# One layer of retention and mixture of experts: the fourth x split sooner, steps 7 to 9 reordered, two x1 tiles on GpSimd

## The chip, the cores and the metric

The kernel runs on one core of a Trainium2 chip. The core has TensorE (PE, with its weight loads PEld), VectorE (DVE), ScalarE (ACT), GpSimd (POOL) and SyncE (SP), which only issues transfers here. The metric is the device time in microseconds.

## The reference

Input x is 16 sequences of 256 tokens with 256 channels. The reference computes, in float32:

```
q, k, v, g = x@w_q+b_q, x@w_k+b_k, x@w_v+b_v, x@w_g+b_g      # 8 heads of 32
q, k = rotated by position (sin, cos)
sim = (q k^T / sqrt(32)) * decay mask (causal, gamma_h ** distance)
ret = group norm of (sim v) per head, * gn_weight + gn_bias
x1  = layernorm(x + (silu(g) * ret) @ w_o + b_o)
logits = x1 @ router_w.T ; the best of 8 experts, score = sigmoid(best logit)
routed = expert MLP of x1*score (256 -> 2*512 -> 256, up * silu(gate))
shared = (silu(x1@sh_gate) * (x1@sh_up)) @ sh_down
out = layernorm(x1 + shared + routed)
```

## The kernel before

The 16 sequences are worked on as 8 pairs of 512 tokens (four tiles of 128). A loop over t runs from 0 to 9; what is done in one turn is called step t here. In step t three pairs are on their way at once: pair t is projected to q, k, v and gate, pair a = t - 1 goes through its similarities, values, group norm and output product, and pair f = t - 2 is layer-normed to x1, turned, put through the shared MLP and routed. Steps 3 to 7 are alike; step 8 has no pair to project (a = 7, f = 6), and step 9 has only the shared MLP of pair 7. After step 9 come 39 slots, each one gather of 128 tokens, one expert's MLP and one scatter.

Every engine has its own list of instructions, written out by hand in the order of its function, and runs it strictly in order; engines wait for each other by semaphores (`wait_ge`). An instruction that waits holds up everything behind it on its engine. There is no planner.

Float32 products are made of three passes of a faster format: a value is split into a high part, copied by ACT, and a low part, which DVE or POOL gets by subtraction. For x this is `x_hi(t)` (ACT) and `x_lo(t)` (DVE, line 1191: x_in minus the high part, both in SBUF). Step t splits the x of pair t + 1, behind the variance; in step 2 alone `x_lo(3)` stands almost at the end (line 1622), behind `y_rest(1)` (line 1278) and in front of `shared_sum(0, ...)` (line 1302) and `output_sum(1)` (line 1315), whose result the similarities of pair 2 (line 1820) wait for. In the same step POOL's list ends with `residual` (line 1020), `turn` (line 977) and `down_rest` (line 1053).

The expert weights are split in the same way in steps 3 to 9: `expert_hi(e)` (ACT, line 811), `expert_lo(e, n)` (DVE, line 1335, waits until n high parts are there) and `expert_rest` (POOL, line 1040). They lie where the projection weights, xT and other buffers of the pairs lie, and so SP's `gate_up_in(e)` waits until those are free.

In step 8 the order is: PE four times similarities and values of pair 7, `x1_transposes(6)` (line 1934), `ret_transposes(7)`, `gate_up_shared(6, ...)` (line 1740) with `y_transposes(7)` (line 2012) and `output(7)` (line 2085) in between, `shared_down(6, 0)` (line 2034), `x1_transposes(7)`, `shared_down(6, 1)`. POOL: `group_rstd(7)` (line 1014), `residual(7)`, four scatters of seats (line 1077), `norm_scales(7)` (last instruction line 1035, semaphore nmr_ok). ACT then writes four tiles of x1 (`first_norm`, line 794), and the high part of x1T (line 743). DVE ends step 8 with `plan_early`, `expert_lo(1, 3)`, `shared_sum(6, 0)`, `x1_lo(7)` (line 1241), `shared_sum(6, 1)`, `expert_lo(2, 4)`; step 9 begins with `shared_product(7, 0)` (line 1287, semaphore h_ok), for which PE waits in front of the fifth of its eight groups `gate_up_shared(7, j, i)`. POOL goes from `norm_scales(7)` to `expert_rest(5, 7)`, which waits for the seventh high part: ACT's `expert_hi(5)`, right behind `x1_hi(7)`.

Of the kernel before, what the change touches and what calls it, by code (L numbers as in the profile page):

```python
# [51 lines left out]
HALF_FF = FF // 2  # L52
PARTED = {1: (0,), 2: (1,), 3: (2,), 4: (3, 4), 5: (5,), 6: (6,), 7: (7,)}
SEATS = (EXPERTS - 1) * TOKENS + SLOTS * P
SEAT = 3
# [7 lines left out]
def build(nc, x, w_q, b_q, w_k, b_k, w_v, b_v, w_g, b_g, w_o, b_o, gn_w, gn_b, router_w,  # L63
          gate_up, down, sh_gate, sh_up, sh_down, x_t, b_qk, w_o_t, b_o_col, rotation, squares, token_seats, free_seats, out):
    ctx = ExitStack()
    with ctx:
# [203 lines left out]
        def x1T_duo(f):  # L270

            return duo[0] if f == PAIRS - 2 else x1_duo(f)

        def v_bank(q):
# [21 lines left out]
        class sig:  # L296
# [68 lines left out]
            lnr_ok = new("lnr_ok")  # L365
            nm_ok = new("nm_ok")
            nmr_ok = new("nmr_ok")
            x1_ok = new("x1_ok")
# [137 lines left out]
        def _(sp):  # L506
# [47 lines left out]
            def step(t):  # L554
# [35 lines left out]
                if has(t - 2) and t < PAIRS:  # L590
                    sums_out(t - 2)
# [85 lines left out]
        def _(act):  # L677
# [76 lines left out]
            def shared_act(f, j):  # L754
                act.wait_ge(sig.gu_ps, 2 * FT * f + 2 * j + 1)
                act.wait_ge(sig.h_ok, at(FT * f + j - 1))
                act.wait_ge(sig.h_rest, at(min(FT * f + j - 1, FT * (PAIRS - 2))))
                nc.scalar.activation(s_act[:, j % 2, :], duo[j % 2][:, 0, :], ACT.Silu).then_inc(sig.sact_ok, 1)

# [37 lines left out]
            def expert_hi(e):  # L797

                act.wait_ge(sig.egu_in[e], 16)
                if e < 2:  # L800
                    act.wait_ge(sig.g_ps, KT * PAIRS)
                    act.wait_ge(sig.xT_lo, KT * PAIRS)
                elif e < 4:
# [32 lines left out]
            for t in range(1, PAIRS + 2):  # L836
# [28 lines left out]
                if has(t) and t > 1:  # L865
                    gate_act(t)
                if has(f):
                    if t == PAIRS:
                        expert_hi(1)
# [16 lines left out]
                if has(f):  # L886
# [9 lines left out]
                    if t == PAIRS:  # L896
                        expert_hi(3)
                    shared_act(f, 3)
# [63 lines left out]
        def _(pool):  # L962
# [124 lines left out]
            for t in range(PAIRS + 2):  # L1087
# [35 lines left out]
                if t == PAIRS:  # L1123
                    norm_scales(a)

            pool.wait_ge(sig.plan_ok, 2)
# [60 lines left out]
        def _(dve):  # L1187
# [93 lines left out]
            def shared_product(f, j):  # L1281
# [4 lines left out]
                to = s_act[:, j % 2, :] if h_parts(f) else hT[:, j, :]  # L1286
                nc.vector.tensor_tensor(to, duo[j % 2][:, 1, :], s_act[:, j % 2, :], ALU.mult)\
                    .then_inc(sig.h_ok, 1)
# [8 lines left out]
            def shared_sum(p, i):  # L1297

                dve.wait_ge(sig.dn_ps, 2 * p + i + 1)
                dve.wait_ge(sig.x1_ok, TILES * (p + 1))  # L1300
                dve.wait_ge(sig.zs_out, 16 * p)
# [23 lines left out]

            def moments(p):
                for q in range(TILES):
                    dve.wait_ge(sig.st_ok, TILES * p + q + 1)
# [15 lines left out]
            def last_products(f):  # L1344

                shared_product(f, 0)
                shared_product(f, 1)
                expert_lo(3, 5)
                for j in range(2, FT):
# [173 lines left out]
            for t in range(1, PAIRS + 2):  # L1523
                a, f = t - 1, t - 2
                if t == 2:
                    products(t, 0)
                    products(t, 1)
                elif has(a):
                    masked(a, 0)
                    if t == PAIRS:  # L1530
                        statistics(f, [0, 1])
                    elif has(f):
                        statistics(f)
                        moments(f)
# [40 lines left out]
                if t == 2:  # L1575
                    swap(t, 1)
                elif has(t + 1) and t != 1:
                    x_lo(t + 1)
                if t == PAIRS + 1:
                    last_products(f)  # L1580
                elif has(f):
# [12 lines left out]
                    else:  # L1594
                        group_norm(a, [0])
                        choose(f)
                        group_norm(a, [1])
                        shared_product(f, 1)
                        go_on(f)
                        find_seats(f)  # L1600
                        gated(a)
                        shared_product(f, 2)
                        for i in range(2):
                            output_sum(a, [i])
                            statistics(a, [2 * i, 2 * i + 1])
                        moments(a)
                    shared_product(f, 3)
                    h_low(f, 3)
                    if t == PAIRS:
                        plan_early()  # L1610

                        dve.wait_ge(sig.nmr_ok, PAIRS)
                        expert_lo(1, 3)
                if has(a) and t < PAIRS:
# [118 lines left out]
        def _(pe):  # L1733
# [66 lines left out]
            def similarities(a, quad):  # L1800
# [3 lines left out]
                if quad == 0:  # L1804

                    pe.wait_ge(sig.v_ok, 2 * (a + 1))
                    if a > 1:
                        pe.wait_ge(sig.gate_ok, KT * (a + 1))
                        pe.wait_ge(sig.z_ok, 2 * (a - 1) + 1)
# [97 lines left out]
            def ret_transposes(a):  # L1907
                pe.wait_ge(sig.ident_in, 16 * 2)
                pe.wait_ge(sig.retT_ok, 2 * (a + 1))

                pe.wait_ge(sig.s_diag, 8 * (a + 1))
                if has(a + 1):
                    pe.wait_ge(sig.prod_ok, 4 * (a + 2))
# [6 lines left out]
            def x1_transposes(f):  # L1920
# [16 lines left out]
                if f == PAIRS - 1:  # L1937
                    for q in range(TILES):
                        pe.wait_ge(sig.x1_ok, TILES * f + q + 1)
                        for k in range(KT):  # L1940
# [34 lines left out]
            def gate_up_shared(f, j, i):  # L1975
                if i == 0:
                    if j == 0:
                        pe.wait_ge(sig.x1T_lo, KT * (f + 1))
                        if f == 0:
                            pe.wait_ge(sig.w_lo, 5)  # L1980
                    if j < 2:

                        if has(f + 2):
                            if j == 0:
                                pe.wait_ge(sig.v_ok, 2 * (f + 3))
                            else:
                                pe.wait_ge(sig.gate_ok, KT * (f + 3))
                        elif has(f + 1):
# [3 lines left out]
                    else:  # L1992
                        pe.wait_ge(sig.h_ok, FT * f + j - 1)
                three(duo[j % 2][:, i, :], lambda part, k: wsgu[:, i, part, k, j * P:(j + 1) * P],
                      lambda part, k: x1T[:, part, k, :], KT).then_inc(sig.gu_ps, 1)
# [27 lines left out]
            def shared_down(f, half):  # L2023
# [14 lines left out]
                if half == 0:  # L2038
# [13 lines left out]
                    down_part(0, [FT - 1])  # L2052
                    down_part(1, range(FT)).then_inc(sig.dn_ps, 1)
                else:
                    down_part(2, [FT - 1])
# [50 lines left out]
            for t in range(1, PAIRS + 2):  # L2106
                a, f = t - 1, t - 2
                if has(a):
                    for n in range(4):
                        if t != 2:  # L2110
                            similarities(a, n)
                            if n:
                                values(a, n - 1)
                        if t == 1 and n == 0:
                            router_of_output()
                        if has(t):
                            project(t, n)
                    if t != 2:
                        values(a, 3)
# [10 lines left out]
                if has(t) and t != 1:  # L2130
                    gate_project(t, [1] if t == 2 else range(KT))
                if t == 1:
# [31 lines left out]
                if has(f):  # L2164
                    shared_down(f, 0)
                    if t == PAIRS:
                        x1_transposes(a)
                    shared_down(f, 1)
                if has(a) and t < PAIRS:
# [190 lines left out]
```

## Time and profile before

| | |
|---|---|
| median of 3 runs | 558.79 us (558.39 to 558.9) |
| the profiled execution | 558.9 us, span 557.1 us |
| PE busy | 537.1 us, 96% of the span, 3830 matmuls |
| DVE, ACT, POOL busy | 414.3, 229.6, 337.7 us |
| mean granted clock | 0.987 |

The profile's times are microseconds from the start of the span. Steps 3 to 7 take some 41.5 us each, with PE busy nearly without a break. The page gives the granted TensorE clock in 40 slices of 13.9 us: it is at 9 (of 10) everywhere but in the seventh slice (from 83.6 us), where it is at 6, and the last.

### The profile page before, as it was taken

Reading aid. Unit: us, or ns where it says so; the run is one execution under the profiler, and the core shown is the slowest. Engines: PE = TensorE matmul, PEld = TensorE weight load, DVE = VectorE, ACT = ScalarE, POOL = GpSimd, SP = SyncE. Lnnn points to the kernel's source line nnn. Section 1 sums busy time; section 2 is a strip of 40 time slices with the busy share of each in tenths; the row PEclk is TensorE's granted clock in tenths of the full one; section 3 lists DMA queues with packets and bytes.
Section 4 is the critical chain, followed back from the end, with each engine's and each line's share of the span. In section 5 each row is a group of like instructions: output and inputs, shape, how many; then the busy total and the mean of one; then the engine's idle time right before and its main releaser. Section 6 shows DMA issues by size and latency. Waiting matters only on the chain.

```text
span 557.1 us, 11796 instructions
## 1 busy us (share of the span) xinstructions
PE 537.1 (96%) x3830; PEld 453.8 (81%) x3830; DVE 414.3 (74%) x892; ACT 229.6 (41%) x410; POOL 337.7 (61%) x330
## 2 busy tenths in 40 slices
PE   8999995999999999999999889999999999999994
PEld 6777894789789789789788678888888888888884
DVE  5896988787987987987977778767866666666664
ACT  4435550355453353353354855133333333333331
POOL 1956674395495385785485385616786556566644
PEclk9999996999999999999999999999999999999998
DMA  8920503403623503603366713855586665565651
GB/s 267 318 94 3 188 3 111 153 2 50 238 94 63 204 1 51 216 1 117 113 251 243 289 53 118 277 181 188 189 195 202 198 189 177 175 198 194 198 181 38
DMA packets 46555, 83.82 MB, mean 150 GB/s; under 512 B 11361, under 2 KB 30577, under 8 KB 46481
## 3 DMA queue, kind: packets, MB, share of 16 engines
q1 hardware_dynamic: 38720, 64.52, 35.0%
q0 software_dynamic: 6112, 15.40, 10.4%
q10 hardware_dynamic: 1664, 3.15, 1.6%
q8 instruction: 33, 0.54, 0.4%
q14 instruction: 26, 0.21, 0.2%
HBM read 61.11 MB, written 22.34 MB: 150 GB/s over the span
## 4 chain that ended last, share of the span: by engine, by line
PE 81%; issue 6%; POOL 5%; DMA 3%; SPq 2%; DVE 2%; ACT 0%; POOLq 0%; DVEq 0%; ACTq 0%
PE duo L1740 46%; PE duo L2199 10%; PE duo L2030 4%; PE duo L1820 3%; PE duo L1845 3%; PE duo L2209 3%; PE duo L1902 3%; PE duo L2034 2%; POOL rstd L1014 2%; PE duo L2020 1%; DMA x_in<-x_t 1%; DMA rot<-rotation 1%; PE duo L2085 1%; PE duo L1934 1%; PE duo L2012 1%
## 5 line engine op out<-in xcount | busy, mean ns | idle before, releaser
L1740 PE MATMUL duo<-w_gu_hi,xsT 128*128 x320 | 107.2, 397 | 0.0
L1740 PE MATMUL duo<-x1T,wsgu 128*128 128x512 f32 x384 | 90.9, 393 | 0.7 <-DVE x1T L1241 0.7
L1740 PEld LDWEIGHTS duo<-x1T,wsgu 128*128 128x128 f32 x384 | 71.4, 188 | 15.9 <-DVE x1T L1241 1.2
L1151 POOL DMA_INDIRECT out_rows<-of,seat x39 | 39.6, 1014 | 56.5 <-DVE of L1697 54.2
L1740 PEld LDWEIGHTS duo<-w_gu_hi,xsT 128*128 128x128 f32 x320 | 59.7, 188 | 11.2
L1740 PE MATMUL duo<-w_gu,xsT 128*128 x160 | 62.0, 387 | 0.0
L1652 DVE SCALAR_TENSOR_TENSOR eh<-duo,seat,e_act 128x512 f32<-128x512 f32 x38 | 28.5, 751 | 40.1 <-PE duo L1740 40.1
L977 POOL TENSOR_TENSOR turned<-turned,swapped 128x1024 f32<-128x1024 f32 x16 | 38.6, 2410 | 30.8 <-DVE swapped L1215 30.8
L1224 DVE TENSOR_TENSOR sims<-duo,causal 128x512 f32<-128x512 f32 x64 | 41.0, 683 | 18.1 <-ACT sims L719 18.0
L719 ACT ACTIVATE sims<-duo 128x256 f32<-128x256 f32 x64 | 21.1, 382 | 74.3 <-PE duo L1820 74.0
L1142 POOL DMA_INDIRECT xz<-xz_d,seat x39 | 45.8, 1174 | 8.9 <-issue 8.7
L1077 POOL DMA_INDIRECT seat_d<-stage,place_i x32 | 36.1, 1127 | 19.8 <-DVE place_i L1483 11.4
L1014 POOL TENSOR_TENSOR rstd<-var_e,minus_half 128x16 f32<-128x16 f32 x16 | 46.4, 2918 | 0.7
L2199 PE MATMUL duo<-w_dn,ehT 128*128 x152 | 46.1, 303 | 0.0
L947 ACT ACTIVATE ehT<-duo 128x512 fp32r<-128x512 f32 x38 | 22.8, 599 | 56.0 <-PE duo L2209 56.0
L2199 PE MATMUL duo<-w_dn,ehT_lo 128*128 x152 | 43.0, 283 | 0.0
L2199 PE MATMUL duo<-dn_rest,ehT 128*128 128x256 f32 x152 | 42.9, 282 | 0.0
L1820 PEld LDWEIGHTS duo<-turned 32*128 32x128 f32 x512 | 26.2, 192 | 17.7 <-issue 15.2
L1740 PE MATMUL duo<-xT,wqk 128*128 128x512 f32 x144 | 40.1, 418 | 0.4
L1820 PE MATMUL duo<-turned 32*128 32x128 f32 (+1 forms) x512 | 33.8, 361 | 6.4 <-DVE x_res L1315 5.9
L940 ACT ACTIVATE e_act<-duo,seat 128x512 f32<-128x512 f32 x38 | 26.2, 690 | 32.3 <-PE duo L1740 32.3
L2030 PE MATMUL duo<-wsd_s,hT_hi 128*128 128x256 f32 x192 | 35.3, 285 | 0.0
(214 smaller groups left out, 1291.7 us busy)
## 6 DMA issues: line engine op xcount, KB each, us to landing
dn_rest<-dn_lo_d SPq DMA_DIRECT2D x39, 512.0 KB
w_gu<-L_ffn_gate_up_proj SPq DMA_DIRECT2D x8, 1024.0 KB, 9.0
x_in<-x_t SPq DMA_DIRECT2D x8, 512.0 KB, 5.4
x_res<-L_attn_x SPq DMA_DIRECT2D x8, 512.0 KB, 4.0
dn_raw<-L_ffn_down_proj SPq DMA_DIRECT2D x8, 512.0 KB, 7.6
dn_hi_d<-dn_top SPq DMA_DIRECT2D x8, 512.0 KB, 4.7
dn_lo_d<-dn_low SPq DMA_DIRECT2D x8, 512.0 KB, 5.4
xz_d<-zs SPq DMA_DIRECT2D x8, 512.0 KB, 4.3
```

Source lines behind the costliest of these rows:

```text
L940: nc.scalar.activation(e_act[:, :], duo[s % 2][:, 0, :], ACT.Silu, scale=f32(seat[:, s, :])[:, 2:3])\
L977: nc.gpsimd.tensor_tensor(turned[:, g, :, :], turned[:, g, :, :], swapped[:, g, :, :], ALU.add)\
L1014: nc.gpsimd.tensor_tensor(rstd[:, half], var_e[:, half], minus_half[:, half], ALU.pow)\
L1077: pool.indirect_dma_start(seat_d, bass.IndirectOffsetOnAxis(ap=place_i[:, q:q + 1], axis=0), stage[:, q, :], None).then_inc(sig.scat, 16)
L1142: pool.indirect_dma_start(xz[:, s % ROWS, :], None, known, bass.IndirectOffsetOnAxis(ap=seat[:, s, 0:1], axis=0))\
L1151: pool.indirect_dma_start(out, bass.IndirectOffsetOnAxis(ap=seat[:, s, 1:2], axis=0), of[:, s % OUTS, :], None).then_inc(sig.out_done[s % ...
L1224: nc.vector.tensor_tensor(sims[:, j % 4, :, 0::2, :], src, mask, ALU.mult).then_inc(sig.s_diag, 1)
L1652: nc.vector.scalar_tensor_tensor(out=eh[:, :], in0=duo[s % 2][:, 1, :], scalar=f32(seat[:, s, :])[:, 2:3], in1=e_act[:, :], op0=ALU.mult, ...
L1740: last = mm(out_, left(a, k), right(b, k), start=start and k == 0 and n == 0, stop=stop and k == kt - 1 and n == len(PASSES) - 1)
L1820: last = mm(sim_duo(a, j)[:, i % 2, SEQ * kb:SEQ * kb + SEQ - P * kb], turned[rows, g, 1, key:key + P], turned[rows, g, 0, key:SEQ * (b + 1)],
L2030: last = mm(duo[2][:, q // 2, D * (q % 2):D * (q % 2 + 1)], left[:, q * P:(q + 1) * P], wsd_s[:, b, n, :], start=n + m == 0, stop=n == FT ...
L2199: last = mm(duo[2][:, 1, 0:D], halves[left][:, f, :], weights[right], start=f + n == 0, stop=f == FT - 1 and n == len(PASSES) - 1)
```

## The change

1. Step 2: DVE does `x_lo(3)` right behind `swap(2, 1)`, where the other steps do it.
2. Pair 7's second half of the gate projection (6 matmuls) and its activation move from step 7 into step 8, in front of the last values (PE) and behind `first_norm(6)` (ACT). Its bank is duo[3].
3. Pair 5's `shared_down` for the fourth tile (12 matmuls) moves from step 7 into step 8, between similarities and values, with DVE's second `shared_sum(5, 1)` and SP's `sums_out(5)`.
4. `gate_up_shared` of pairs 5, 6 and 7 starts its first group with the four matmuls that need only the high part of x1T; for pair 6 the banks are swapped, so that its first group doesn't write the bank from which x1T is read.
5. DVE in step 8: the statistics come one place sooner, `go_on` stands before the second half of `group_norm`, the moments come in two halves, `x1_lo(7)` comes before `shared_sum(6, 0)`.
6. Expert weights: `gate_up_in(0)` waits only for the q and k projections, `gate_up_in(1)` comes in step 8; experts 1 and 3 change places in the lists of ACT and DVE.
7. Pair 7's x1: ACT writes tiles 0 and 1, POOL tiles 2 and 3 right behind `norm_scales(7)`, with a semaphore of their own, x1_rest, which PE, DVE and SP wait for.

The diff, without the declarations and the waits that only follow from these points:

```diff
@@ gate_bank, gu_duo
-            if t == 0:
+            if t == 0 or t == LATE and k:            # LATE = PAIRS - 1
                 return duo[3][:, k, :]
+        def gu_duo(f, j):
+            return duo[(j + (f == PAIRS - 2)) % 2]   # used by gate_up_shared, shared_act, shared_product
@@ SP, step(t)
+                if t - 1 == LATE:
+                    sums_out(t - 3)
                 if has(t - 2):
-                    sp.wait_ge(sig.x1_ok, TILES * (t - 1))
+                    sp.wait_ge(sig.x1_ok, TILES * (t - 1) - 2 * (t > PAIRS))
+                    if t > PAIRS:
+                        sp.wait_ge(sig.x1_rest, 2)
...
                 if t == PAIRS - 1:
-                    sp.wait_ge(sig.g_ps, KT * PAIRS)
+                    sp.wait_ge(sig.qk_ps, 4 * PAIRS)
                     gate_up_in(0)
-                    gate_up_in(1)
...
                 if t == PAIRS:
-                    sp.wait_ge(sig.o_ps, 2 * (PAIRS - 1))
-                    gate_up_in(7)
                     sp.wait_ge(sig.s_ps, 8 * PAIRS)
                     gate_up_in(2)
+                    sp.wait_ge(sig.o_ps, 2 * (PAIRS - 1))
+                    sp.wait_ge(sig.g_ps, KT * PAIRS)
+                    gate_up_in(1)
+                    gate_up_in(7)
@@ ACT
-                    first_norm(f, [TILES - 1] if 2 < t < PAIRS else range(TILES))
+                    first_norm(f, [TILES - 1] if 2 < t < PAIRS else range(2 if t > PAIRS else TILES))
+                if t == PAIRS:
+                    gate_act(a, [1])
...
-                    gate_act(t)
+                    gate_act(t, [0] if t == LATE else range(KT))
@@ POOL
                 if t == PAIRS:
                     norm_scales(a)
+                    pool.wait_ge(sig.nmr_ok, PAIRS)
+                    for q in range(2, TILES):
+                        nc.gpsimd.tensor_scalar(x1_last[:, q, :], x_res[:, q, :], ln_r[:, q:q + 1], nmr[:, q:q + 1],
+                                                ALU.mult, ALU.add).then_inc(sig.x1_rest, 1)
@@ DVE
+                    if t == PAIRS:
+                        statistics(f, [0, 1])
                     masked(a, 0)
                     if t == PAIRS:
-                        statistics(f, [0, 1])
+                        statistics(f, [2, 3])
+                        moments(f)
...
                     masked(a, 1)
-                    if t == PAIRS:
-                        statistics(f, [2, 3])
-                        moments(f)
...
+                    if t - 1 == LATE:
+                        shared_sum(f - 1, 1)
                     masked(a, 3)
...
                 if t == 2:
                     swap(t, 1)
-                elif has(t + 1) and t != 1:
+                if has(t + 1) and t != 1:
                     x_lo(t + 1)
...
                         choose(f)
+                        go_on(f)
                         group_norm(a, [1])
                         shared_product(f, 1)
-                        go_on(f)
...
-                if t == 2:
-                    x_lo(t + 1)
+                if t == PAIRS:
+                    x1_lo(a)
                 if has(f):
                     shared_sum(f, 0)
-                    if t == PAIRS:
-                        x1_lo(a)
-                    if t <= PAIRS:
+                    if t <= PAIRS and t != LATE:
                         shared_sum(f, 1)
@@ PE, gate_up_shared
+                if f >= LATE - 2 and i + j == 0:
+                    for n in (0, 2, 1):
+                        part, low = PASSES[n]
+                        if low:
+                            pe.wait_ge(sig.x1T_lo, KT * (f + 1))
+                        for k in range(KT):
+                            last = mm(gu_duo(f, 0)[:, 0, :], wsgu[:, 0, part, k, 0:P], x1T[:, low, k, :],
+                                      start=n + k == 0, stop=low == 1 and k == KT - 1)
@@ PE, step 8
                             if n:
+                                if t == PAIRS and n == 2:
+                                    shared_down(f - 1, 2)
                                 values(a, n - 1)
+                            elif t == PAIRS:
+                                shared_down(f - 1, 1)
...
+                    if t == PAIRS:
+                        gate_project(a, [1])
                     if t != 2:
                         values(a, 3)
```

## Rows read from the trace of the kernel before

**Rows 1.** PE timeline, steps 3, 4, 5 begin: start, us, instruction [idle before]

```profile
92.43 1.66 PE L1820 MATMUL duo<-turned 32*128 32x256 f32 x16 [5.89 <-DVE x_res L1315]
...
136.68 0.94 PE L1820 MATMUL duo<-turned 32*128 32x256 f32 x16
...
178.21 0.94 PE L1820 MATMUL duo<-turned 32*128 32x256 f32 x16
```

**Rows 2.** 2 us stretches: length, busy PE, PEld, DVE, ACT, POOL, PEclk, DMA, GB/s

```profile
88.00:90.00 2.00, 0.00 (x0) 0.00 (x0) 2.00 (x1) 0.00 (x0) 1.74 (x1) 0.68 0.00 0
...
96.00:98.00 2.00, 2.00 (x15) 1.20 (x17) 1.41 (x8) 0.00 (x0) 0.49 (x3) 0.50 1.02 416
98.00:100.00 2.00, 2.00 (x30) 1.20 (x23) 1.00 (x2) 0.66 (x2) 1.10 (x2) 0.76 1.02 383
```

**Rows 3.** DVE timeline, steps 2 and 6: start, us, instruction, count

```profile
68.61 0.69 DVE L1287 TENSOR_TENSOR s_act<-duo,s_act 128x512 f32<-128x512 f32 x1 [0.79 <-PE duo L1740]
...
80.49 1.36 DVE L1278 TENSOR_TENSOR yT_lo<-yT,yT_hi 128x512 fp32r<-128x512 f32 x2
81.77 8.53 DVE L1191 TENSOR_TENSOR xT<-x_in,xT 128x512 fp32r<-128x512 f32 x2
...
241.98 1.29 DVE L1191 TENSOR_TENSOR xT<-x_in,xT 128x512 fp32r<-128x512 f32 x2 [0.86 <-ACT xT L696]
```

**Rows 4.** POOL timeline, the same two places

```profile
82.71 2.41 POOL L1020 TENSOR_TENSOR x_res<-x_res,bias_o 128x1024 f32<-128x1024 f32 x1
...
87.40 2.34 POOL L1053 TENSOR_TENSOR dn_low<-dn_raw,dn_top 128x1024 fp32r<-128x1024 f32 x1
...
241.60 5.80 POOL L1014 TENSOR_TENSOR rstd<-var_e,minus_half 128x16 f32<-128x16 f32 x2
```

**Rows 5.** PE timeline of step 8

```profile
311.52 0.86 PE L1845 MATMUL duo<-sims,v 128*32 128x256 f32 x16 [0.83 <-DVE sims L1224]
...
315.09 7.09 PE L1740 MATMUL duo<-x1T,wsgu 128*128 128x512 f32 x30 [0.70 <-DVE x1T L1241]
...
323.39 1.09 PE L2012 MATMUL duo<-ident,y 128*128 128x128 f32 x8 [0.89 <-DVE y L1261]
...
328.02 3.80 PE L2085 MATMUL duo<-wo,yT 128*128 128x264 f32 x16 [0.76 <-issue]
```

**Rows 6.** ACT timeline of step 8

```profile
310.31 2.07 ACT L794 ACTIVATE x<-x_res,nmr,ln_r 128x256 f32<-128x256 f32 x4
...
338.75 1.08 ACT L743 ACTIVATE x1T<-duo 128x512 fp32r<-128x512 f32 x2 [0.99 <-PE duo L1934]
339.73 3.72 ACT L811 ACTIVATE w_gu_hi<-w_gu 128x2048 fp32r<-128x2048 f32 x2
```

**Rows 7.** DVE timeline of steps 8 and 9

```profile
336.72 2.28 DVE L1335 TENSOR_TENSOR w_gu<-w_gu,w_gu_hi 128x2048 fp32r<-128x2048 f32 x1
...
341.63 2.28 DVE L1335 TENSOR_TENSOR w_gu<-w_gu,w_gu_hi 128x2048 fp32r<-128x2048 f32 x1
...
347.24 3.31 DVE L1335 TENSOR_TENSOR w_gu<-w_gu,w_gu_hi 128x2048 fp32r<-128x2048 f32 x1
```

**Rows 8.** POOL timeline of steps 8 and 9

```profile
332.25 0.97 POOL L1077 DMA_INDIRECT seat_d<-stage,place_i  x1 [0.30 <-issue]
...
335.32 0.33 POOL L1035 TENSOR_TENSOR nmr<-nm,ln_r 128x4 f32<-128x4 f32 x1
341.78 6.61 POOL L1040 TENSOR_TENSOR w_gu<-w_gu,w_gu_hi 128x2048 fp32r<-128x2048 f32 x1 [6.12 <-ACT w_gu_hi L811]
```

**Rows 9.** POOL line 1040: ns min/median/max, first and last start

```profile
L1040 POOL TENSOR_TENSOR w_gu<-w_gu,w_gu_hi x2: 4584/5596/6608, 225.8 to 341.8; 128x2048 fp32r<-128x2048 f32 x2
```

**Rows 10.** the chain that ended last, around step 9: start, us, what

```profile
337.95 0.87 PE duo L1934 x8
338.83 2.16 PE duo L2034 x10
340.99 11.04 PE duo L1740 x48
```

More of the change, by code:

```diff
@@ L53 @@
 PARTED = {1: (0,), 2: (1,), 3: (2,), 4: (3, 4), 5: (5,), 6: (6,), 7: (7,)}
+LATE = PAIRS - 1
 SEATS = (EXPERTS - 1) * TOKENS + SLOTS * P
@@ L366, in build @@
             nm_ok = new("nm_ok")
+            x1_rest = new("x1_rest")
             nmr_ok = new("nmr_ok")
@@ L589, in step @@
                     down_raw_in(PARTED[t][1])
-                if has(t - 2) and t < PAIRS:
+                if has(t - 2) and t < LATE:
                     sums_out(t - 2)
@@ L757, in shared_act @@
                 act.wait_ge(sig.h_rest, at(min(FT * f + j - 1, FT * (PAIRS - 2))))
-                nc.scalar.activation(s_act[:, j % 2, :], duo[j % 2][:, 0, :], ACT.Silu).then_inc(sig.sact_ok, 1)
+                nc.scalar.activation(s_act[:, j % 2, :], gu_duo(f, j)[:, 0, :], ACT.Silu).then_inc(sig.sact_ok, 1)
             def h_high(f, j):
@@ L896, in _ @@
                     if t == PAIRS:
[L897 removed]
+                        expert_hi(1)
                     shared_act(f, 3)
@@ L1299, in shared_sum @@
                 dve.wait_ge(sig.dn_ps, 2 * p + i + 1)
-                dve.wait_ge(sig.x1_ok, TILES * (p + 1))
+                dve.wait_ge(sig.x1_ok, TILES * (p + 1) - 2 * (p == PAIRS - 1))
+                if p == PAIRS - 1:
+                    dve.wait_ge(sig.x1_rest, 2)
                 dve.wait_ge(sig.zs_out, 16 * p)
@@ L1324, in statistics, with moments @@
                     nc.vector.bn_stats(stats[:, q, :], x_res[:, q, :]).then_inc(sig.st_ok, 1)
-            def moments(p):
-                for q in range(TILES):
+            def moments(p, tiles=range(TILES)):
+                for q in tiles:
                     dve.wait_ge(sig.st_ok, TILES * p + q + 1)
@@ L1347, in last_products @@
                 shared_product(f, 1)
-                expert_lo(3, 5)
+                expert_lo(1, 5)
                 for j in range(2, FT):
@@ L1605, in _ @@
                             statistics(a, [2 * i, 2 * i + 1])
-                        moments(a)
+                            moments(a, [2 * i, 2 * i + 1])
                     shared_product(f, 3)
@@ L1612, in _ @@
                         dve.wait_ge(sig.nmr_ok, PAIRS)
-                        expert_lo(1, 3)
+                        expert_lo(3, 3)
                 if has(a) and t < PAIRS:
@@ L1911, in ret_transposes @@
                 pe.wait_ge(sig.s_diag, 8 * (a + 1))
+                if a == LATE:
+                    pe.wait_ge(sig.gate_ok, KT * PAIRS)
                 if has(a + 1):
@@ L1938, in x1_transposes @@
                     for q in range(TILES):
-                        pe.wait_ge(sig.x1_ok, TILES * f + q + 1)
+                        if q < 2:
+                            pe.wait_ge(sig.x1_ok, TILES * f + q + 1)
+                        else:
+                            pe.wait_ge(sig.x1_rest, q - 1)
                         for k in range(KT):
@@ L1977, in gate_up_shared @@
                     if j == 0:
-                        pe.wait_ge(sig.x1T_lo, KT * (f + 1))
+                        if f < LATE - 2:
+                            pe.wait_ge(sig.x1T_lo, KT * (f + 1))
+                        else:
+                            pe.wait_ge(sig.x1T_hi, KT * (f + 1))
                         if f == 0:
@@ L1993, in gate_up_shared @@
                         pe.wait_ge(sig.h_ok, FT * f + j - 1)
-                three(duo[j % 2][:, i, :], lambda part, k: wsgu[:, i, part, k, j * P:(j + 1) * P],
+                if f >= LATE - 2 and i + j == 0:
+                    for n in (0, 2, 1):
+                        part, low = PASSES[n]
+                        if low:
+                            pe.wait_ge(sig.x1T_lo, KT * (f + 1))
+                        for k in range(KT):
+                            last = mm(gu_duo(f, 0)[:, 0, :], wsgu[:, 0, part, k, 0:P], x1T[:, low, k, :],
+                                      start=n + k == 0, stop=low == 1 and k == KT - 1)
+                    last.then_inc(sig.gu_ps, 1)
+                    return
+                three(gu_duo(f, j)[:, i, :], lambda part, k: wsgu[:, i, part, k, j * P:(j + 1) * P],
                       lambda part, k: x1T[:, part, k, :], KT).then_inc(sig.gu_ps, 1)
@@ L2053, in shared_down @@
                     down_part(1, range(FT)).then_inc(sig.dn_ps, 1)
+                    if f == LATE - 2:
+                        down_part(2, [FT - 1])
+                elif f == LATE - 2:
+                    if half == 1:
+                        down_part(3, [0])
+                    else:
+                        down_part(3, range(1, FT)).then_inc(sig.dn_ps, 1)
                 else:
@@ L2130, in _ @@
                 if has(t) and t != 1:
-                    gate_project(t, [1] if t == 2 else range(KT))
+                    gate_project(t, [1] if t == 2 else [0] if t == LATE else range(KT))
                 if t == 1:
@@ L2167, in _ @@
                         x1_transposes(a)
-                    shared_down(f, 1)
+                    if t != LATE:
+                        shared_down(f, 1)
                 if has(a) and t < PAIRS:
```

9 lines of the change are left out of this document (5 added, 4 removed).

## The prediction

> **What bounds the kernel now.** I read the page first: TensorE is busy in 96% of the span and 81% of the last chain is its own, so the time falls only where PE waits or runs slowly, and its work is not changed. The slices of the granted clock then show one dip. PE's timeline there has the only long wait of the run: at 92.43 PE has stood 5.89 us for line 1315, so the output product before it was over at 86.54 [rows 1]. The windows show what followed. The granted clock, at the higher of its two levels (2.4 GHz) until then, is 0.68 on average in 88 to 90: 0.72 us at full and 1.28 at half speed (1.2 GHz), so it fell at 88.7, about 2.2 us into the wait; it is still 0.50 in 96 to 98 and is back in 98 to 100 [rows 2]. Step 3 therefore took 136.68 - 92.43 = 44.25 us where step 4 took 178.21 - 136.68 = 41.53 [rows 1]: 2.7 us for the clock alone.
>
> The cause is in DVE's timeline: the two subtractions x_lo(3) took 8.53 us, the same two in step 6 took 1.29 [rows 3]. In that time GpSimd ran three tensor operations without a break, from 82.71 to 89.74 [rows 4], and DVE went on half a microsecond after the last. So a DVE operation with both inputs in SBUF stands still while GpSimd works on SBUF tensors. The same pair meets at step 9: expert_lo takes 3.31 instead of 2.28 from 347.24 on, until just after GpSimd's line 1040 ends at 348.39 [rows 7, 8], and line 1040 takes 6.61 us there, 4.58 elsewhere [rows 9], because expert_lo had started 0.15 us before it [rows 7, 8]. The one that begins first runs, the other waits. GpSimd's powers on 16 columns are no such obstacle: x_lo of step 6 ran beside them in 1.29 us [rows 3, 4].
>
> Last, step 8 (302.8 to 341): PE has short waits there, of 0.83, 0.70, 0.89 and 0.76 us [rows 5], and some stretched similarities. From 341 on PE doesn't wait until the slots, which the change leaves alone.
>
> **Step 2 (the sooner x_lo).** At its new place, at about 67.8, DVE meets GpSimd's powers, as in step 6, and takes 1.29 us. It stands before a product that waited 0.79 us for PE anyway [rows 3], and half a microsecond of delay ends at the second half of the group norm, which waits for GpSimd's powers. The end of y_rest stays at 80.49 + 1.36 = 81.85, before 82.71, where GpSimd's three begin [rows 3, 4]. Behind it come only sums and masks that read PSUM and one SBUF operand. So output_sum follows the output product directly and PE starts step 3 at 86.6, not 92.43: -5.8 us. With no wait the clock stays: -2.7. Together -8.5 us. Below that, a quarter of a microsecond may be lost if a statistic meets down_rest, at most 0.7; above, nothing.
>
> **Step 7.** 18 matmuls leave it: 6 of the gate (1.4 us), 12 of the down projection (1.4). PE would be 2.8 sooner; but the products of the shared MLP hang on the second group norm, which hangs on the powers, which don't move. Followed through DVE and ACT, the output product starts 2.0 us sooner. SP: gate_up_in(0) goes out about 8 us sooner, gate_up_in(1) about 30 later, at 313, with 2 and 7 behind it, needed from 325 on; hidden.
>
> **Step 8.** The 2.8 us of PE work come back between similarities and values, into the 0.83 us wait [rows 5] and into issues stretched by waits for masks. DVE's chain of masks, statistics and one more sum (0.7) is about as long as PE's. I get the values' end, and x1_transposes, 0.7 us sooner than before (-2.0 + 2.8 - 1.5). ACT has the gate (0.6) more behind its four tiles of x1 [rows 6], so the high part of x1T is out at 313.7; the first group starts there, not after the low part: 313.75 against 315.09 [rows 5], -1.35. The chain over squares, variance and powers is bound by ACT and gains only 0.55, so y_transposes come at 322.8 against 323.39: PE waits some 1.7 us in all here, where it waited 0.89 [rows 5]. Behind that, go_on no longer stands still beside residual, and gated is done in time: the 0.76 us wait for the output product [rows 5] goes. Output starts 1.6 us sooner. What costs nothing here: the changed order of experts (their waits on ACT are long over), the split moments (-0.2 us on DVE, but GpSimd comes from its scatters later than that).
>
> **The two x1 tiles on GpSimd.** ACT's four took 2.07 us [rows 6]. GpSimd's scatters end at 333.22 [rows 8]; they follow the powers and gain 0.55, and with the wait behind them gone nmr is there at 334.6 (335.65 before, [rows 8]). PE wants the tiles from 336.4 on (337.95 - 1.6, [rows 10]). With ACT alone the last would be there at 336.7, as its transposes are reached at 337.0. So this part gains nothing on PE. A tile of 256 columns costs GpSimd 4.58 / 8 = 0.57 us by its two-input operation [rows 9], with 0.15 for its start 0.7; half of that, 0.35, if one input is twice as fast, and 0.95 if the two scalars slow it down. I take 0.7, the nearest row's: done at 336.2. In this time DVE comes to expert_lo (335.1; 336.72 before, [rows 7]) and finds GpSimd at work: it starts at 336.2, ends at 338.5. x1_lo(7) is done at 339.8; PE's first four matmuls of step 9 (339.4 to 340.3) cover that. So step 9 starts on PE at 339.4, -1.6 us.
>
> **The new wait in step 9.** GpSimd's line 1040 starts behind ACT's x1T and one high part: 341.78 - 338.82 = 2.96 us after PE's last x1 transpose [rows 6, 8, 10], now at 340.2. DVE's expert_lo(2) started 341.63 - 338.82 = 2.81 us after it [rows 7, 10], and so just first. Now it has x1_lo(7) (1.3) and two sums (1.2) behind the late expert_lo: 338.5 + 2.5 = 341.0. GpSimd is first by 0.8 us; it works 4.58 us [rows 9] to 344.8, then expert_lo 2.28 to 347.05, then the first product 0.65: 347.7. PE, after four groups of 1.36 (11.04 / 48 x 6 = 1.38, [rows 10]), needs that product at 339.4 + 5.45 = 344.85. It stands for 2.9 us: +2.9. Behind DVE's waiting expert_lo is all of the shared MLP of pair 7. What GpSimd does sooner then (the gathers) nobody waits for.
>
> A page of the Trainium skill, "SBUF — State Buffer", section "Who interferes with whom", says that the one of the two engines that starts first holds the shared port for its whole instruction and that the other fully blocks; the rows here fit that, but DVE in step 2 was held through three instructions [rows 3, 4], not one. By the page's wording alone x_lo would have gone in after 2.4 us; for step 9, where GpSimd has one instruction, both give the same 2.9.
>
> The page "GPSIMD Engine Reference", section "Engine selection", calls GpSimd roughly as fast as the line rate with one input. Then both x1 tiles would be done soon after 335.2, expert_lo(3) hardly late, and the meeting in step 9 a draw, as in the first rival. No row here shows such an instruction at this size.
>
> **Sum**, against the profiled execution's own 558.9 us (span 557.1, 1.8 around it): -5.8 - 2.7 - 1.6 + 2.9 = -7.2, so 551.7. The median of the runs is 0.1 below this execution: 551.6.
>
> **Rivals.**
> A. No new wait. expert_lo(2) is first, as before, or GpSimd's tiles are short. For it: without any delay of expert_lo(3), DVE would come to expert_lo(2) 2.96 to 3.0 us after the x1 transposes, a draw. Against: x1_lo(7) before the two sums makes that 0.15 later than before even then. Time: 551.6 - 2.9 = 548.7.
> B. The new wait takes the clock too. For it: it fell 2.2 us into the long wait [rows 2], and this one is 2.9. Against: the waits below 1 us never did it, and 2.9 may miss it. The half speed cost 2.7 us in step 3 [rows 1]: 551.6 + 2.7 = 554.3.
> C. Slower: in step 2 GpSimd's residual (82.71) catches y_rest instead. It decides at 81.15: if GpSimd is there before the second subtraction starts, 1.5 us sooner than now, y_rest ends at 90.4, the output product starts then and step 3 at 93.5, 1.1 later than before with the same clock; with +1.3 from steps 7 to 9 that is 561.2. Against: GpSimd's scatters there wait for DVE's place_i, which doesn't move.
> D. The rework of steps 7 and 8 gives nothing in itself, PE's chain there being held by ACT and the powers: 551.6 + 1.6 = 553.2. For it: the only wait over half a microsecond that the moved work fills is that of 0.83 us [rows 5]. Against: the x1T wait and the one for the output are truly removed.
>
> **How the numbers follow.** Forecast 0.42, A 0.27, B 0.18, D 0.08, C 0.03, 0.02 for something else. The likeliest one's own range is 550.5 to 552.8. Eight in ten: from 547.8 (A with a quarter of a microsecond less per GpSimd tile and all of step 7's 2.8) to 554.8 (B with a tile 0.5 late). What a measurement of this kernel can tell is about 0.2%, 1.1 us. Faster by more than that (below 557.7): 0.95; within: 0.02; slower: 0.03.
>
> **What would show it.** Right: no PE wait at line 1820 and no dip of the clock near 90, x_lo in step 2 in 1.3 us, step 3 in 41.5; step 9's first eight groups with a wait of nearly 3 us at the fifth, put down to DVE's hT product, with an expert_lo of 6 us in front of it, GpSimd's subtraction of 4.6 instead of 6.61. Wrong: an expert_lo of 2.28 there and PE unbroken means A; a granted clock at one half after it, B; a long y_rest or statistics in step 2, C. If x1_rest holds up PE's transposes by over half a microsecond, my price for GpSimd's tile is too low. The whole fails if step 3 is still 44 us long.

## The result: 1.4% faster, nearly all of it from one moved pair of subtractions

| kernel | median us | runs from to | to the kernel before, 95% interval |
|---|---|---|---|
| changed | 550.51 | 550.29 to 551.69 | 0.9861, 0.9844 to 0.9878 |
| changed, once more on another occasion | 550.88 | 550.39 to 551.28 | 0.9864, 0.9847 to 0.9880 |
| before, beside the first | 558.59 | 557.92 to 558.90 | |

The profiled execution of the changed kernel took 551.69 us (span 549.9), 1.2 more than its others; 7.2 less span than before. The mean granted clock rose from 0.987 to 0.997.

PE's timeline of the changed kernel where steps 3 and 4 begin (start, us, instruction), against [rows 1]:

```profile
86.73 0.94 PE L1840 MATMUL duo<-turned 32*128 32x256 f32 x16
...
128.26 0.94 PE L1840 MATMUL duo<-turned 32*128 32x256 f32 x16
```

Step 3 begins at 86.73 instead of 92.43, with no wait (-5.70), and takes 128.26 - 86.73 = 41.53 us instead of 44.25 (-2.72): -8.4 in all. The stretch in which the clock had fallen [rows 2], now:

```profile
88.00:90.00 2.00, 2.00 (x19) 1.47 (x20) 1.89 (x5) 0.36 (x2) 2.00 (x1) 1.00 1.18 46
```

DVE in step 2, against [rows 3]: x_lo(3) (now line 1209) at its new place, and y_rest (now line 1296), behind which nothing stands still any more:

```profile
67.99 1.26 DVE L1209 TENSOR_TENSOR xT<-x_in,xT 128x512 fp32r<-128x512 f32 x2
...
80.75 1.36 DVE L1296 TENSOR_TENSOR yT_lo<-yT,yT_hi 128x512 fp32r<-128x512 f32 x2
```

PE in steps 8 and 9, against [rows 5, 10] (line 1956 is x1_transposes, 2051 y_transposes, 2131 the output product, 2029 the split first group):

```profile
303.77 1.09 PE L1956 MATMUL duo<-ident,x 128*128 128x128 f32 x8
...
305.61 1.66 PE L2029 MATMUL duo<-x1T,wsgu 128*128 128x512 f32 x6
...
314.75 1.09 PE L2051 MATMUL duo<-ident,y 128*128 128x128 f32 x8 [0.90 <-DVE y L1279]
...
318.46 3.72 PE L2131 MATMUL duo<-wo,yT 128*128 128x264 f32 x16
...
328.13 0.82 PE L1956 MATMUL duo<-ident,x_last 128*128 128x128 f32 x6
330.23 0.44 PE L1956 MATMUL duo<-ident,x_last 128*128 128x128 f32 x2 [1.27 <-POOL x_last L1141]
...
332.47 1.74 PE L2029 MATMUL duo<-x1T,wsgu 128*128 128x512 f32 x6
```

The output product starts 9.56 us sooner than at 328.02: 1.1 from the rework, beyond the 8.4. The last two transposes of pair 7 then wait 1.27 us for GpSimd's second tile, and step 9 starts at 332.47, where before it started at 340.85:

```profile
340.85 11.18 PE L1740 MATMUL duo<-x1T,wsgu 128*128 128x512 f32 x48
```

That is 8.4 sooner, so the rework has given its gain back. GpSimd (1049 ends norm_scales, 1141 is the two tiles, 1054 the subtraction of expert 5), against [rows 8], and line 1141's instances apart (ns min/median/max, first and last start):

```profile
326.64 0.20 POOL L1049 TENSOR_TENSOR nmr<-nm,ln_r 128x4 f32<-128x4 f32 x1
326.95 3.22 POOL L1141 TENSOR_SCALAR x_last<-x_res,ln_r,nmr 128x256 f32<-128x256 f32 x2
333.62 6.76 POOL L1054 TENSOR_TENSOR w_gu<-w_gu,w_gu_hi 128x2048 fp32r<-128x2048 f32 x1 [3.45 <-ACT w_gu_hi L823]
```

```profile
L1141 POOL TENSOR_SCALAR x_last<-x_res,ln_r,nmr x2: 573/1614/2654, 327.0 to 327.5; 128x256 f32<-128x256 f32 x2
```

The first tile took 0.57 us, the second 2.65. DVE, against [rows 7]:

```profile
327.12 0.43 DVE L1412 CAST slot_ri<-slot_row 128x21 int32<-128x21 f32 x1
327.46 2.28 DVE L1355 TENSOR_TENSOR w_gu<-w_gu,w_gu_hi 128x2048 fp32r<-128x2048 f32 x1
...
331.22 1.29 DVE L1259 TENSOR_TENSOR x1T<-duo,x1T 128x512 fp32r<-128x512 f32 x2 [1.48 <-ACT x1T L754]
...
333.62 2.28 DVE L1355 TENSOR_TENSOR w_gu<-w_gu,w_gu_hi 128x2048 fp32r<-128x2048 f32 x1
335.85 0.69 DVE L1305 TENSOR_TENSOR hT<-duo,s_act 128x512 f32<-128x512 f32 x1
```

The cast at 327.12 took 0.43 us where it takes 0.17, held by the first tile; then expert_lo(3) ran its 2.28 us and the second tile was the one that stood still, until 329.7. At 333.62 DVE's expert_lo(2) and GpSimd's subtraction came together to within 0.01 us; DVE ran (2.28), GpSimd stood (6.76), the product followed at 335.85, and PE didn't wait. This near tie came out the same way in all five profiles that have it (two of the changed kernel, and those of the four tiles on ACT and of the two kernels with moved matmuls back); in two of them GpSimd is even recorded 0.01 us ahead (332.24 against 332.25, 332.05 against 332.06). A last 0.6 us of this one execution, a wait of PE at 412 for gathered rows of a later slot, is not in the profile of the other occasion.

### The profile page after: what moved, and what is told of

It reads as the page before. It is cut to its first block and busy times, and to the rows that moved or that the text cites. A ratio compares the mean times of both kernels' runs of the same rounds, so it can differ in the third digit from the quotient of the medians.

```text
span 549.9 us, 11803 instructions
## 1 busy us (share of the span) xinstructions
PE 535.8 (97%) x3830; PEld 451.9 (82%) x3830; DVE 406.6 (74%) x892; ACT 228.1 (41%) x408; POOL 341.0 (62%) x332
## 5 line engine op out<-in xcount | busy, mean ns | idle before, releaser
L1760 PE MATMUL duo<-x1T,wsgu 128*128 128x512 f32 x366 | 86.9, 392 | 0.4 <-DVE hT L1305 0.4
L1760 PEld LDWEIGHTS duo<-x1T,wsgu 128*128 128x128 f32 x366 | 68.1, 188 | 14.9 <-DVE hT L1305 0.9
L1760 PE MATMUL duo<-xT,wqk 128*128 128x512 f32 x144 | 38.8, 408 | 0.5
L1760 PEld LDWEIGHTS duo<-w_gu,xsT 128*128 128x128 f32 x160 | 30.2, 189 | 5.2
L1840 PEld LDWEIGHTS duo<-turned 32*128 32x128 f32 x512 | 25.0, 184 | 10.7 <-issue 8.6
```

The source lines that it names most:

```text
L1760: last = mm(out_, left(a, k), right(b, k), start=start and k == 0 and n == 0, stop=stop and k == kt - 1 and n == len(PASSES) - 1)
L1840: last = mm(sim_duo(a, j)[:, i % 2, SEQ * kb:SEQ * kb + SEQ - P * kb], turned[rows, g, 1, key:key + P], turned[rows, g, 0, key:SEQ * (b + 1)],
```

## The experiments

**Only the sooner x_lo.** The kernel before, with this edit alone:

```diff
-                elif has(t + 1) and t != 1:
+                if has(t + 1) and t != 1:
                     x_lo(t + 1)
...
-                if t == 2:
-                    x_lo(t + 1)
```

> The kernel before with the one edit of step 2: x_lo(3) behind swap(2, 1). Theory 1 (all of the gain is the wait and the half clock of steps 2 and 3): 558.6 - 8.3 = 550.3 us, the wait of 5.9 us and the dip of the clock gone, steps 8 and 9 as in the kernel before, so the whole rework of steps 7 to 9 is worth about nothing. Theory 2 (the rework gives the 1.6 us that I had put down for steps 7 and 8): 552 us and more. Theory 3 (GpSimd's three operations then stop another DVE instruction of step 2): over 554 us.

Measured: 550.42 us (549.95 to 551.34), ratio 0.9856 (0.9841 to 0.9872). That is the changed kernel's time: theory 1 holds, and steps 7 to 9 as changed are worth nothing together. Its meeting in step 9, DVE and then GpSimd, is the one of before:

```profile
333.65 2.28 DVE L1335 TENSOR_TENSOR w_gu<-w_gu,w_gu_hi 128x2048 fp32r<-128x2048 f32 x1
```

```profile
333.80 6.61 POOL L1040 TENSOR_TENSOR w_gu<-w_gu,w_gu_hi 128x2048 fp32r<-128x2048 f32 x1 [6.13 <-ACT w_gu_hi L811]
```

**All four x1 tiles on ACT.** The changed kernel, with

```diff
-first_norm(f, ... range(2 if t > PAIRS else TILES))
+first_norm(f, ... range(TILES))       # tiles 2 and 3 signal x1_rest
-                    for q in range(2, TILES):
-                        nc.gpsimd.tensor_scalar(x1_last[:, q, :], ...).then_inc(sig.x1_rest, 1)
```

> The changed kernel with all four x1 tiles of pair 7 on ACT again. Theory 1 (the second tile on GpSimd, 2.65 us where the first took 0.57, stood still for DVE's expert_lo and held PE up by 1.27 us): the wait in front of the last x1 transposes goes or falls below 0.4 us, 1 us faster than the changed kernel, 549.5. Theory 2 (ACT's four are as late): no change, 550.5. Theory 3 (the meeting of expert_lo(2) and GpSimd's line 1054 in step 9 turns the other way, since DVE and GpSimd come to it within 0.01 us in the changed kernel): a wait of 2.9 us in step 9, 552 or more.

Measured: 549.43 us (548.76 to 549.82), ratio 0.9840 (0.9826 to 0.9853); beside it on the same chip the sooner x_lo alone had 549.95 at the least (median 550.42). Theory 1: the eight transposes run with hardly a wait (1.28 us for 1.04),

```profile
328.00 1.28 PE L1952 MATMUL duo<-ident,x_last 128*128 128x128 f32 x8
```

and the rework is worth 1.0 us once GpSimd's tiles are out of it.

**The tiles first.** The changed kernel, with one wait more in front of expert_lo(3):

```diff
                         dve.wait_ge(sig.nmr_ok, PAIRS)
+                        dve.wait_ge(sig.x1_rest, 2)
                         expert_lo(3, 3)
```

> The changed kernel with one wait more: DVE's expert_lo(3) of step 8 waits until GpSimd's two tiles are written. Theory 1 (the lock is what made the second tile late): both tiles take 0.57 us, PE's wait of 1.27 us goes, expert_lo(3) ends 0.6 us later. Then DVE's next expert_lo comes to GpSimd's line 1054 no sooner than GpSimd: if GpSimd is first, PE waits up to 2.9 us in step 9 and the time is 552; if DVE is first, 549.3. Theory 2 (a tensor_scalar of this size is slow on GpSimd by itself): the second tile is still over 1.5 us and the time is 550.5 or more.

Measured: 553.37 us (552.16 to 553.58), ratio 0.9905 (0.9890 to 0.9920). Both halves of theory 1 came true. GpSimd's tiles took 1.12 us together and its next subtraction was first, undisturbed:

```profile
326.83 1.12 POOL L1141 TENSOR_SCALAR x_last<-x_res,ln_r,nmr 128x256 f32<-128x256 f32 x2
332.00 4.62 POOL L1054 TENSOR_TENSOR w_gu<-w_gu,w_gu_hi 128x2048 fp32r<-128x2048 f32 x1 [4.05 <-ACT w_gu_hi L823]
```

DVE's expert_lo(2) came 0.64 us later, and PE stood in front of the fifth group of step 9:

```profile
332.64 6.12 DVE L1355 TENSOR_TENSOR w_gu<-w_gu,w_gu_hi 128x2048 fp32r<-128x2048 f32 x1
```

```profile
339.42 7.31 PE L1761 MATMUL duo<-x1T,wsgu 128*128 128x512 f32 x24 [2.74 <-DVE hT L1305]
```

This is the wait that I had predicted for the changed kernel. In stretches of 2 us (the columns are those of [rows 2]) the granted clock fell at 339.5, as PE took up its work again, and was at one half for 3.4 us:

```profile
338.00:340.00 2.00, 0.58 (x2) 0.49 (x3) 2.00 (x4) 0.00 (x0) 1.72 (x1) 0.87 0.52 144
340.00:342.00 2.00, 2.00 (x6) 1.61 (x5) 2.00 (x1) 0.00 (x0) 1.98 (x1) 0.50 0.75 243
342.00:344.00 2.00, 2.00 (x8) 1.57 (x8) 0.16 (x1) 0.60 (x1) 1.70 (x2) 0.77 0.22 39
```

**DVE later by 1.2 us.** The changed kernel, with two reductions of PSUM, whose result is unused, in front of the last sum of step 8:

```diff
+                        ...                            # two waits, for PE and GpSimd
+                        for i in range(2):
+                            nc.vector.tensor_reduce(var[:, 16 * i:16 * i + 16], duo[2][:, i, :]..., X, ALU.add)
                         shared_sum(f, 1)
```

> The changed kernel with two reductions of PSUM more on DVE, 1.2 us together, in front of the last sum of step 8; their result is not used. They make DVE come to expert_lo(2) about 1.2 us behind GpSimd's line 1054. Theory 1 (whichever of the two starts first holds the other for its whole length): line 1054 takes 4.6 us instead of 6.76, expert_lo some 5.7, and PE waits 2.5 to 3 us in front of the fifth group of step 9: 3 us slower than the changed kernel, 553.5; if such a wait also takes the clock, 556. Theory 2 (DVE gets the port in any case, at most a piece of an instruction late): 1.2 us of DVE time behind which PE hardly waits, 550.5 to 551.5.

Measured: 554.91 us (553.06 to 556.77), ratio 0.9945 (0.9927 to 0.9963). Theory 1: GpSimd first, DVE's 2.28 us become 5.57, PE waits 2.75.

```profile
333.05 4.62 POOL L1054 TENSOR_TENSOR w_gu<-w_gu,w_gu_hi 128x2048 fp32r<-128x2048 f32 x1 [3.45 <-ACT w_gu_hi L823]
```

```profile
334.25 5.57 DVE L1355 TENSOR_TENSOR w_gu<-w_gu,w_gu_hi 128x2048 fp32r<-128x2048 f32 x1
```

Its five executions differ more than those of any other kernel here: 553.06 and 553.67 with a mean granted clock of 0.997, 554.91 and 555.52 with 0.994, 556.77 with 0.991. Only the first has a trace: PE waits 2.75 us, and the clock doesn't fall. That the slower ones lost it at this wait is what their means suggest; it is not shown.

**The product first.** The kernel with the tiles first, and DVE's first product of step 9 in front of expert_lo(2):

```diff
                 shared_product(f, 0)
+                expert_lo(2, 4)
                 shared_product(f, 1)
...
                         shared_sum(f, 1)
                     if t == PAIRS:
-                        expert_lo(2, 4)
+                        pass
```

> The kernel with the tiles first (expert_lo(3) waits for GpSimd's two tiles), in which expert_lo(2) lost to GpSimd by 0.6 us and PE stood 2.7 us, with shared_product(7, 0) in front of expert_lo(2). Theory 1 (the stall came from the product behind the held expert_lo): the wait of 2.7 us goes, at most 0.5 us stays in front of the seventh group, 549.3 to 550. Theory 2 (PE's wait has another cause, such as the later x1T): still over 552.

Measured: 549.32 us (549.13 to 549.83), ratio 0.9839 (0.9824 to 0.9855): 4 us from one moved instruction. Some 1.6 of them are the clock: the 24 matmuls behind the wait took 7.31 us with the tiles first and 5.73 with DVE later, where the clock stayed. expert_lo is still held (3.95 us), but behind the product it costs PE only some 0.3 us:

```profile
333.90 0.69 DVE L1305 TENSOR_TENSOR hT<-duo,s_act 128x512 f32<-128x512 f32 x1 [1.52 <-PE duo L1762]
334.51 3.95 DVE L1355 TENSOR_TENSOR w_gu<-w_gu,w_gu_hi 128x2048 fp32r<-128x2048 f32 x1
```

**The same order, tiles on ACT**, and the changed kernel beside it:

> The changed kernel with all four x1 tiles on ACT, and with DVE's shared_product(7, 0) in front of expert_lo(2) instead of behind it. Theory 1 (the product is all that PE waits for behind the meeting with GpSimd's line 1054, and the meeting was won by DVE): 549.4 us as with the four tiles alone; the order only takes away the risk. Theory 2 (the later expert_lo(2) now loses against GpSimd and pushes shared_product(7, 1) and what is behind it): a new wait of up to 1.5 us in front of the seventh group of step 9, 550.5 or more.

> The changed kernel once more, unedited, beside the next ones on the same chip, as their measure. 550.5 us by all theories (0.986 of the kernel before).

Measured: 549.85 us (549.38 to 549.95), ratio 0.9844 (0.9831 to 0.9858), against 550.88 (550.39 to 551.28): 1.0 faster, the same as with the four tiles alone. GpSimd now comes first (332.30 against DVE's 335.14) and PE has no long wait: the order protects against a lost meeting and doesn't gain.

**x_lo in front of y_rest.** The kernel before, with the two last subtractions of step 2 exchanged:

```diff
+                if t == 2:
+                    x_lo(t + 1)
                 if in_parts(a):
                     y_rest(a)
-                if t == 2:
-                    x_lo(t + 1)
```

> The kernel before with x_lo(3) of step 2 moved in front of y_rest(1) only, so that y_rest's second subtraction starts at about 82.4, where x_lo's second did. Theory 1 (any DVE operation with both inputs in SBUF is held there by GpSimd's three operations): x_lo takes 1.3 us, y_rest 8 us and more, PE waits 7 us in front of the output product; 559.5 to 561, slower than the kernel before, my rival C. Theory 2 (it is something of x_lo itself, its buffers or its place): 550.3, as with the sooner x_lo.

Measured: 559.12 us (558.44 to 560.20), ratio 1.0019 (1.0008 to 1.0029), 1.1 us slower than the kernel before (557.98 beside it). The 8.5 us went over from one operation to the other:

```profile
80.25 1.29 DVE L1191 TENSOR_TENSOR xT<-x_in,xT 128x512 fp32r<-128x512 f32 x2
81.45 8.52 DVE L1278 TENSOR_TENSOR yT_lo<-yT,yT_hi 128x512 fp32r<-128x512 f32 x2
```

```profile
90.22 0.78 PE L1740 MATMUL duo<-wo_s,yT_hi 128*128 128x264 f32 x2 [6.73 <-DVE yT_lo L1278]
```

The clock was at one half from 86.7 to 93.5, so PE did the output product slowly and began step 3 at 94.78; from there on it ran at full speed.

The trace also shows that the order of the starts doesn't settle who is held. In the kernel before, x_lo(3)'s two subtractions:

```profile
L1191 DVE TENSOR_TENSOR xT<-x_in,xT x2: 689/4309/7929, 81.8 to 82.4; 128x512 fp32r<-128x512 f32 x2
```

The second is recorded from 82.37 on, 0.34 us ahead of GpSimd's first operation (82.71), and yet it took 7.93 us and ended 0.56 us behind GpSimd's last operation, when nearly all of its own 0.69 us was still to be done. Here y_rest's second subtraction did the same (from 82.11 on, GpSimd from 82.45), and so did x_lo's with down_rest later (82.62, 82.96). In step 9 of the kernel before DVE started 0.15 us ahead and ran. What differs is not shown; in step 2 GpSimd was busy with its scatters until 0.02 us before, in step 9 it had been waiting.

**down_rest later.** The kernel before, with GpSimd's third operation of the row moved behind norm_scales(1) in step 3:

```diff
+                if t == 3:
+                    down_rest(PARTED[2][-1])
...
-                if t in PARTED:
+                if t in PARTED and t != 2:
                     down_rest(PARTED[t][-1])
```

> The kernel before with GpSimd's down_rest(1) moved from the end of step 2 into step 3, behind norm_scales(1). Two operations then stand in a row behind the scatters of step 2, not three. Theory 1 (DVE's x_lo(3) is held until GpSimd's row of operations ends): x_lo ends at 87.9 and not at 90.2, PE's wait is 3.6 us and not 5.9; 2.3 us faster than the kernel before if the clock falls as before, 556, and up to 5 us faster if it doesn't. Theory 2 (something else, the fetching of instructions or x_lo's buffers, ends the standstill): no change.

Measured: 555.29 us (554.70 to 556.34), ratio 0.9945 (0.9928 to 0.9962). Theory 1: x_lo takes 6.24 us instead of 8.53 and ends half a microsecond behind GpSimd's second operation (87.70), with no third to wait for,

```profile
82.02 6.24 DVE L1193 TENSOR_TENSOR xT<-x_in,xT 128x512 fp32r<-128x512 f32 x2
```

```profile
85.33 2.37 POOL L977 TENSOR_TENSOR turned<-turned,swapped 128x1024 f32<-128x1024 f32 x1
```

PE waits 3.60 us, and the clock is down for 3.4 us instead of some 10:

```profile
88.00:90.00 2.00, 0.00 (x0) 0.00 (x0) 2.00 (x5) 0.00 (x0) 0.00 (x0) 1.00 0.00 0
90.00:92.00 2.00, 1.61 (x19) 1.43 (x20) 1.05 (x4) 0.65 (x2) 0.00 (x0) 0.99 0.79 250
92.00:94.00 2.00, 2.00 (x8) 1.15 (x11) 2.00 (x6) 0.01 (x1) 0.00 (x0) 0.50 1.06 217
94.00:96.00 2.00, 2.00 (x32) 1.20 (x28) 0.99 (x7) 0.66 (x2) 1.26 (x3) 0.66 0.14 57
```

**The moved matmuls back.** The kernel with four tiles on ACT, with both pieces of moved PE work back in step 7 (parts 2 and 3 of the change undone), and with the gate alone back (part 2):

```diff
-                    if t == PAIRS:
-                        gate_project(a, [1])
...
-                                if t == PAIRS and n == 2:
-                                    shared_down(f - 1, 2)
```

> The kernel with ACT's four tiles, and in it the 18 moved matmuls (pair 7's second half of the gate with its activation, pair 5's fourth tile of shared_down with its sum) back in step 7. What is left of the rework is the split first group, the swapped banks, go_on, the order of the statistics and of the experts. Theory 1 (the moved work fills PE's waits in step 8 and is what gains 1 us over the sooner x_lo alone): 550.4 us. Theory 2 (the moved work comes back in full, and the split of x1T and go_on gain): 549.4 as with it, or less.

> The kernel with ACT's four tiles, with only the 6 gate matmuls and their activation back in step 7; shared_down's 12 stay in step 8. Theory 1 (the activation, 0.67 us on ACT between the four x1 tiles and x1T, stands on the chain to the powers): y_transposes 0.5 us sooner in step 8, but step 7 longer by 0.9 to 1.4, 549.8 in all. Theory 2 (step 7's end is held by the powers anyway, the gate goes back for nothing): 549.0.

Measured: both back 549.93 us (549.61 to 550.19), ratio 0.9849 (0.9835 to 0.9862); gate back 549.38 (549.20 to 549.78), 0.9838 (0.9825 to 0.9851). So moving the down projection is worth 0.5 us, barely clear of the spread (the ranges overlap), and moving the gate nothing that shows. With the gate back PE waited 1.01 us for the last values. Its profile beside that of the four tiles alone, each counted from its own step 1's similarities (42.00 and 42.26): ACT's tiles of x1 began 0.45 us later (301.34 and 301.15), and the high part of x1T only 0.07 later (304.16 and 304.35). So what ACT saved in step 8 had been spent in step 7. Neither theory of the first fits in full; both pieces together bring about half of the 1.0 us. The rest lies in what was left of the rework (the split first group, go_on, the orders on DVE and of the experts); which of them brings it was not tested.

## Why the prediction was right, and where it wasn't

- **Step 2 and the clock, -8.5.** Right in mechanism and size: -5.70 and -2.72 in the profile, and 558.24 - 550.42 = 7.8 us with that edit alone. (In that kernel's profile step 4 begins 8.0 us sooner, at 128.64, because already step 1's similarities came 0.6 later, at 42.80 and not 42.17.) That DVE is held by GpSimd is shown by two moves: what stands at x_lo's place is held in its stead, and a row of GpSimd operations that is one shorter holds it 2.3 us less.
- **Steps 7 and 8, -1.6.** Right in kind, half as high again as measured: 1.1 in the profile at the output product, 1.0 in the time once the tiles are on ACT. The wait of 0.76 us in front of the output product went, as forecast. The chain over the powers was mis-sized: y_transposes come 0.2 us sooner (314.75 against 323.39, less the 8.4), not 0.55.
- **The two tiles on GpSimd, "this part gains nothing on PE".** Too kind: it cost 1.3 us. I had priced the tile at 0.7 us (0.57 alone, so right) and made DVE the one that waits through both tiles, as in step 2. DVE got its turn between the two tiles, and the second tile waited for all of expert_lo. The prediction's own sign (a hold-up by x1_rest of over half a microsecond means that the price is too low) would have misled: the price was right, and what was wrong is which of the two engines would be held.
- **The new wait in step 9, +2.9.** This step failed. It rested on expert_lo(3) being 1.1 us late and on that delay reaching expert_lo(2). expert_lo(3) was some 0.3 us late (327.46; 327.06 with four tiles on ACT, the output product 0.14 sooner there), and DVE then stood 1.48 us for ACT's x1T anyway, behind PE's late last transpose. From that transpose the arrivals of both DVE and GpSimd are counted; so they arrived together, and DVE ran. That is rival A, whose "draw" it was, in a form that I had not foreseen: the wait missing, but its 2.9 us half replaced by the 1.3 of the tile. The price itself was sound: 2.74 and 2.75 us in the two kernels that made GpSimd first.
- **The sum.** -7.2 forecast, -8.1 measured by the medians. That it lies so near is partly luck, owed to errors of opposite sign (+2.9 not there, +1.3 and +0.5 not foreseen); the likeliest case itself, with the new wait, did not come about.
- **Rivals B and C** are both real, as kernels of their own: B in the tiles-first kernel (in the DVE-later one its wait is shown, the loss of the clock only suggested), C in the exchanged order (559.12; my 561.2 had the new wait of step 9 in it). There step 3 began at 94.78 and not at 93.5, but with the clock back at full speed, which I had not reckoned with.
- **The rule "the one that begins first runs".** It fits step 9 and fails in step 2, the main case: x_lo's second subtraction is recorded 0.34 us before GpSimd's first operation and was held. One reading was loose: DVE's expert_lo of 347.24 stood until GpSimd's line 1040 ended at 348.39, but itself ended only at 350.55.

The page "SBUF — State Buffer" of the Trainium skill, section "Who interferes with whom", says the port is held for one whole instruction. At the tiles this case agrees (DVE's cast and expert_lo went in between two tiles); in step 2 DVE was held through three operations (though it is recorded as starting first), and through two when one was moved. What makes the difference is open.

## What to carry to other kernels

A DVE instruction with both inputs in SBUF may be held by GpSimd's tensor operations for as long as these follow one another; look in a trace for one whose longest instance is many times the median, and put it where GpSimd does small work or none. Where two such operations meet anyway, a few tenths of a microsecond decide which one is held (GpSimd ahead by 0.6 us: DVE; both together: GpSimd), and not always by who is recorded first; so put first on DVE what another engine waits for, and the long subtraction that has time behind it. Offloading a short tile to GpSimd beside a running DVE stream can cost a whole DVE instruction: here 2.28 us for 0.57 us of work.

## What was not expected of the hardware

- GpSimd's multiply-add of one 128x256 tile with two scalars per partition takes 0.57 us alone, as ACT's 0.52.
- The clock: with a wait of 5.89 us half speed lasted about 10 us from 88.7 on, with one of 6.73 us 6.8 (86.7 to 93.5), with one of 3.60 us 3.4, with 2.74 us 3.4, and with 2.75 us in another kernel there was none. So the longest wait didn't cost the longest stretch. At 3.60 and 2.74 us it fell only when PE was at work again (by 1.6 and 0.1 us).
- DVE was held through two and three of GpSimd's operations in a row in step 2, though it is recorded as starting 0.34 us before them, but not through two tiles in step 8.
